# Layer 0 attention: a head's output projection in two stacked products instead of three, a DMA filling the upper half of the second operand

## What is computed

```python
kv_nope, kv_rope = (kv[..., :KV_LORA], kv[..., KV_LORA:])     # KV_LORA = 64
kvu = (kv_nope @ Wkv_up.T + bkv_up).reshape(b, s, NH, QK_NOPE + V_HEAD)...
scores = jnp.einsum('bhqd,bhkd->bhqk', q, k) / np.sqrt(Q_HEAD)
attn = jax.nn.softmax(scores, axis=-1)
o = jnp.einsum('bhqk,bhkv->bhqv', attn, v)
out = jnp.einsum('bhsv,Hv->bsH', o, Wo) + bo
```

## Time and profile before

| | |
|---|---|
| device time, median of 3 runs | 1565.31 us (1564.77 to 1566.88) |
| span of the profiled execution | 1564.7 us |
| time beside the span | no time of its own is listed for the profiled execution; its span lies 0.1 us under the fastest run |
| TensorE busy | 1503.2 us, 96% of the span |
| VectorE, ScalarE, GpSimd busy | 70%, 49%, 30% |
| attention heads of layer 0 | first scores at 39 us, last projection at 403 us |

### The profile page before, as it was taken

The page is one execution under the profiler, slowest core; times in us unless marked ns, Lnnn a source line. Parts: engine busy times, 40 slices in busy tenths (PEclk is TensorE's granted clock), DMA queues, the critical chain, the costliest instruction groups (busy, mean ns, idle before and its releaser), DMA issues. The chain is left out here.

```text
span 1564.7 us, 29168 instructions
## 1 busy us (share of the span) xinstructions
PE 1503.2 (96%) x9057; PEld 1320.1 (84%) x9057; DVE 1098.6 (70%) x2790; ACT 771.0 (49%) x2153; POOL 475.6 (30%) x505
## 2 busy tenths in 40 slices
PE   6999999999689989999999999999999999999898
PEld 5899999998367777888889888888888888988776
DVE  3788888888486756666676666666666667666765
ACT  3777878787345534434444444344443444444521
POOL 3445454545231013113213213312311321321321
PEclk9999999999799999999999999999999999999999
DMA  4111111111144440111011011011011101100001
GB/s 162 37 57 46 55 48 53 52 49 46 55 140 145 133 148 8 48 54 39 15 54 54 0 54 54 0 54 54 12 41 54 44 9 54 54 0 13 1 14 41
DMA packets 42833, 80.20 MB, mean 51 GB/s; under 512 B 5040, under 2 KB 13744, under 8 KB 42800
## 3 DMA queue, kind: packets, MB, share of 16 engines
q1 hardware_dynamic: 42800, 79.77, 16.8%
HBM read 77.66 MB, written 2.10 MB: 51 GB/s over the span
## 5 line engine op out<-in xcount | busy, mean ns | idle before, releaser
L98 PE MATMUL c_bj<-g_xT_hi,b_w 128*128 128x512 f32 x512 | 214.6, 419 | 2.8 <-PEq L901 2.8
L99 PE MATMUL c_bj<-g_xT_lo,b_w 128*128 128x512 f32 x512 | 203.3, 397 | 0.0
L100 PE MATMUL c_bj<-g_xT_hi,b_w 128*128 128x512 f32 x512 | 203.0, 397 | 0.0
L438 POOL TENSOR_TENSOR h_pr<-h_pr,h_rinv 128x512 f32<-128x512 f32 x128 | 133.2, 1041 | 159.9 <-DVE h_rinv L529 157.5
L1119 POOL CAST b_w<-b_raw_q 128x512 fp32r<-128x512 f32 x32 | 20.5, 640 | 435.8 <-PE c_bj L100 435.8
L98 PE MATMUL c_bj<-b_w,g_xT_hi 128*128 128x256 f32 x512 | 143.2, 280 | 0.0
L99 PE MATMUL c_bj<-b_w,g_xT_hi 128*128 128x256 f32 x512 | 143.2, 280 | 0.0
L100 PE MATMUL c_bj<-b_w,g_xT_lo 128*128 128x256 f32 x512 | 142.7, 279 | 0.0
L468 ACT ACTIVATE h_pr<-h_bs,h_nmax 128x256 f32<-128x256 f32 x256 | 118.8, 474 | 3.0 <-DVE h_nmax L524 2.1
L1351 DVE TENSOR_TENSOR c_v_lo<-c_bj,c_v_hi 128x256 fp32r<-128x256 f32 x128 | 54.3, 424 | 93.9 <-ACT c_v_hi L1263 93.9
L1247 ACT ACTIVATE c_o<-c_bo 128x128 f32<-128x128 f32 x128 | 35.5, 277 | 171.2 <-PE c_bo L1465 171.2
(11 more groups left out here) (266 smaller groups left out, 4663.8 us busy)
## 6 DMA issues: line engine op xcount, KB each, us to landing
f_wi<-in_w_ffn SPq DMA_DIRECT2D x66, 256.0 KB, 2.6
h_part<-in_w_ffn SPq DMA_DIRECT2D x32, 264.0 KB, 2.8
b_raw_q<-in_w_attn SPq DMA_DIRECT2D x32, 256.0 KB, 6.8
b_raw_k<-in_w_attn SPq DMA_DIRECT2D x32, 256.0 KB, 7.3
b_raw_v<-in_w_attn SPq DMA_DIRECT2D x16, 512.0 KB, 7.6
b_raw_o<-in_w_attn SPq DMA_DIRECT2D x16, 512.0 KB, 3.9
a_w<-in_w_head SPq DMA_DIRECT2D x32, 225.0 KB, 2.8
e_wraw<-in_w_ffn SPq DMA_DIRECT2D x1, 2304.0 KB, 8.4
```

The lines of the kernel that those rows point to most:

```text
L98: pe.matmul(out, w[0], x[0], start=start, stop=False, skip_group_check=True)
L99: pe.matmul(out, w[0], x[1], start=False, stop=False, skip_group_check=True)
L100: return pe.matmul(out, w[1], x[0], start=False, stop=stop, skip_group_check=True)
L438: pool.tensor_tensor(pr[b][:, :, :], pr[b][:, :, :], rinv[b][:, :][:, :, None].to_broadcast([P, 2, S]), ALU.mult)\
```

## The change

Each projection becomes two products. The first is hi times hi over all 128 rows, as before. The second uses two stacked operands: `wv_mix` has the rounded weights in rows 0 to 63 and their remainder in rows 64 to 127, and `o{i}_mix` has the remainder of the output's rows 0 to 63 in its lower half and a copy of the rounded rows 0 to 63 in its upper half. So hi times lo and lo times hi are added in one product. The cross terms of rows 64 to 127 (which are themselves a lo part) are left out. The copy across partitions is a DMA from `o_hi` to `o_mix`, issued by SyncE. Projections move from rounds b0 and b2 to b1 and b3, and `split_wv` from b1 to b2.

```diff
-        wvs = (t.sb("wv_hi", [P, VH], F32R), t.sb("wv_lo", [P, VH], F32R))
+        wvs = (t.sb("wv_hi", [P, VH], F32R), t.sb("wv_mix", [P, VH], F32R))
...
-        o = [(t.sb(f"o{i}_hi", [P, HALF], F32R), t.sb(f"o{i}_lo", [P, HALF], F32R)) for i in range(2)]
+        o = [(t.sb(f"o{i}_hi", [P, HALF], F32R), t.sb(f"o{i}_mix", [P, HALF], F32R)) for i in range(2)]
...
             round_(NH + 1, 0)
+            round_(NH + 1, 1)
...
                 def fetch_wv(h):
-                    need(sp, s_wvl, h)
+                    need(sp, s_wvl, 2 * h)
...
-                def both(h):
-                    fetch(h + 1)
-                    fetch_wv(h)
-                    fetch_part(h)
-
-                loop(sp, NH - 1, both)
-                fetch_wv(NH - 1)
-                fetch_part(NH - 1)
+                def duplicate(p, par):
+                    sp.wait_ge(s_ohi, p + 1)
+                    sp.dma_start(f32(o[par][1][KVL:P, :]), f32(o[par][0][0:KVL, :])).then_inc(s_odup[par], 16)
+
+                def ahead(h):
+                    if has(h - 3, NH):
+                        duplicate(2 * h - 6, 0)
+                    if has(h, NH):
+                        fetch(h)
+                    if has(h - 2, NH):
+                        fetch_wv(h - 2)
+                    if has(h - 3, NH):
+                        duplicate(2 * h - 5, 1)
+                    if has(h - 1, NH):
+                        fetch_part(h - 1)
+
+                fetch(1)
+                fetch_part(0)
+                ahead(2)
+                with sp.Fori(3, NH) as h:
+                    ahead(h)
+                for h in range(NH, NH + 3):
+                    ahead(h)
...
-                    pool.tensor_tensor(wvs[1][:, :], wv[:, :], f32(wvs[0][:, :]), ALU.subtract).then_inc(s_wvl, 1)
+                    plain(pool, s_tick)
+                    pool.tensor_copy(wvs[1][0:KVL, :], wv[0:KVL, :]).then_inc(s_wvl, 1)
+                    pool.wait_ge(s_wvl, 2 * h + 1)
+                    pool.tensor_tensor(wvs[1][KVL:P, :], wv[KVL:P, :], f32(wvs[0][KVL:P, :]), ALU.subtract)\
+                        .then_inc(s_wvl, 1)
+                    pool.wait_ge(s_wvl, 2 * h + 2)
...
-                    if b == 1 and has(h - 1, NH):
+                    if b == 2 and has(h - 1, NH):
                         split_wv(h - 1)
...
-                    dve.tensor_tensor(o[par][1][:, :], bo[:, :], f32(o[par][0][:, :]), ALU.subtract)\
+                    dve.tensor_tensor(o[par][1][0:KVL, :], bo[0:KVL, :], f32(o[par][0][0:KVL, :]), ALU.subtract)\
                        .then_inc(s_olo, 1)
...
-                    pe.wait_ge(s_wvl, h + 1)
-                    matmul3(pe, acc[c][:, :], (wvs[0][:, :], wvs[1][:, :]), (o[c][0][:, :], o[c][1][:, :]), False,
-                            False).then_inc(s_om, 1)
+                    pe.wait_ge(s_odup[c], 16 * (h + 1))
+                    pe.wait_ge(s_wvl, 2 * h + 2)
+                    pe.matmul(acc[c][:, :], wvs[0][:, :], o[c][0][:, :], start=False, stop=False,
+                              skip_group_check=True)
+                    pe.matmul(acc[c][:, :], wvs[1][:, :], o[c][1][:, :], start=False, stop=False,
+                              skip_group_check=True).then_inc(s_om, 1)
...
-                    if b == 0 and has(h - 2, NH):
+                    if b == 1 and has(h - 2, NH):
                         project(h - 2, 2 * h - 3, 1)
-                    if b == 2 and has(h - 1, NH):
+                    if b == 3 and has(h - 1, NH):
                         project(h - 1, 2 * h - 2, 0)
```

More of the change, by code:

```diff
@@ L372, in attention0_heads @@
         s_pv, s_ohi, s_olo = k.sem("pv"), k.sem("o_hi"), k.sem("o_lo")
-        s_wvh, s_wvl, s_om = k.sem("wv_hi"), k.sem("wv_lo"), k.sem("om")
+        s_wvh, s_wvl, s_om = k.sem("wv_hi"), k.sem("wv_mix"), k.sem("om")
+        s_odup = [k.sem(f"o_dup{i}") for i in range(2)]
         def run(eng, round_):
```

## The result

The changed kernel takes 1575.89 us (median of 4 runs), against 1565.8 us for the kernel before in the same comparison: 1.0057 times, 95% interval 1.0042 to 1.0072, or about +9 us. The change makes the kernel slower; the forecast was +6.4 us, to 1571.7 us. Both medians, 1575.9 us and 1574.4 us in the second comparison, lie inside the range of 1567.5 to 1576.5 us, the first near its upper end.

The account below looks back on a forecast made before the run. ScalarE's exponentials were taken to hold round b2 at 2.34 us, TensorE's work the other rounds. Loop +6.8, head 1 +0.5 and tail -0.9 gave +6.4 us, 1571.7 us; range 1567.5 to 1576.5 us, about 0.8.

Parts of the forecast that it names:

- The limit of round b2: Round b2: b3's scores wait for ScalarE's exponentials, so it stays 2.34 us and removing its 0.70 us projection wins nothing.
- the chain: ScalarE in b2: query rounding, probability rounding, then exponentials, 2.09 us from 0.20 us after the round's start; unmoved by the change.
- The faster rival: Round b2: exponentials don't hold b3, so the hole closes; 1554.7 us, or 1550 to 1552 with no limit; chance 0.10.
- Rounds b1 and b3 pay in full: Each gains two products, 0.47 us, with nothing else bounding its length: b1 3.36 us, b3 3.35 us.
- Round b0 wins its 0.70 us: Round b0 loses its projection and falls from 3.00 to 2.30 us, the normalization being ready just in time.
- The second rival: Round b0's transposes wait for GpSimd's normalization, the margin being 0.02 us: 0.1 us a pass, +2.9 us, 1574.6 us; chance 0.10.
- The pass: One loop pass of four rounds: 11.35 us against 11.11; over 29 passes +6.8 us.
- The copies and the split: Copies inside SBUF land after 2.1 us, the longer weight split takes at most 1.3 us; neither is waited for in the loop.
- The clock: Idle times in each pass lower TensorE's granted clock to 0.98 in the loop: up to 6.6 us, 1578 us; chance 0.03.
- The tail: Behind the loop: -0.6 earlier transposes, -1.28 last values, +1.4 copy wait, -0.43 product saved; together -0.9 us.
- The sum: Whole kernel: 6.8 + 0.5 - 0.9 = +6.4 us on a 1564.7 us span, plus 0.6 for the median: 1571.7 us.
- the likeliest case: Whole kernel: one added product a pass, end of the head stage as forecast; 1569 to 1574.5 us; chance 0.68.

Follow-up runs that it names:

- second comparison: The changed kernel, nothing edited, timed once more against the kernel before: 1.0045 (1.0032 to 1.0058); the kernel before against itself gave 1.0002.
- the repeat: The kernel before, nothing edited, run and profiled once more against itself: 1.0002 (0.9992 to 1.0011).
- second pair: Profiles of the kernel before and the changed kernel, both run again with nothing edited: 1.0002 and 1.0045 of the kernel before.

## Why the prediction was right

**The limit of round b2.** Right, and the step on which all hangs. I had read 2.34 us from rows 4 and 5; it is 2.34 in the changed kernel, with three products moved, and with the projection left out, and falls by 0.49 us when the chain becomes 0.49 us shorter. It is shown from both sides. The faster rival, that TensorE alone sets the pace, is out: 96 products could be taken away without effect.

**Rounds b1 and b3 pay in full.** Right: 3.35 us were measured for each, for the 3.36 and 3.35 predicted.

**Round b0 wins its 0.70 us.** Right: 2.32 or 2.30 us for 2.30. No wait on the normalization is listed there, so the margin of 0.02 us held; with so thin a margin that is in part luck. The second rival didn't come, though the run without b0's projection shows the wait where I had placed it.

**The pass.** 11.36 for 11.35 us. Up to the start of head 31 TensorE is 7.6 us behind the kernel before (391.37 against 383.74), where my sum had 7.3.

**The copies and the split.** Right. 2.2 us to landing where I took 2.1, between the rows of the loads; the estimate from the Trainium skill ("DMA: Bandwidth & Descriptors", anatomy of one DMA), 2.3 us, lies as far from it on the other side, though the section states its fit for DMAs that GpSimd issues and SyncE issues this one. Neither the copies nor the split is waited for in the loop. The third GpSimd instruction takes 0.29 us on 64 rows, my upper bound.

**The clock.** The rival didn't come: with 0.6 to 0.8 us idle in each pass the granted clock was 1.00 from 200 to 300 us.

**The tail.** The mis-sized term. I said -0.9 us. In the first pair of profiles it is -2.1 us: 7.6 us behind at head 31, and 5.6 us (409.31 against 403.74) at the first read of the sums. In the second pair it is -0.3 us: 7.5 us behind at head 31 (391.59 against 384.07), and 7.3 us (409.54 against 402.28) at the end. What parts the two pairs is TensorE's clock in the kernel before. The first read of the sums and the last 7.7 us of the head stage, in its first profile:

```profile
403.74 1.26 ACT L701 ACTIVATE o_os<-a_acc,g_bvs 128x512 f32<-128x512 f32 x2 [2.73 <-PEq L389]
...
396.00:403.70 7.70, 4.64 (x14) 3.26 (x14) 1.98 (x3) 1.60 (x3) 0.00 (x0) 0.62 0.00 0
```

and in the repeat, with the first product of the last projection, which had 0.79 us in the earlier trace rows:

```profile
401.01 0.50 PE L98 MATMUL a_acc<-h_o_hi,h_wv_hi 128*128 128x512 f32 x1 [1.41 <-DVE h_o_lo L538]
...
402.28 1.27 ACT L701 ACTIVATE o_os<-a_acc,g_bvs 128x512 f32<-128x512 f32 x2 [2.04 <-PEq L389]
...
394.60:402.30 7.70, 3.96 (x22) 2.98 (x22) 1.98 (x3) 1.70 (x4) 1.13 (x3) 1.00 0.00 0
```

The same code had a granted clock of 0.62 once and of 1.00 once. From the start of head 31 to the first read of the sums it takes 20.00 us in the first profile and 18.21 in the repeat; in the changed kernel it takes 17.94 and 17.95. The step that I had wrong is that I took the low clock of one profile for a property of the place, and priced there the projection that delayed the last values (1.28 us) and the product saved (0.43 us). Where both kernels ran at the full clock, in the second pair, the parts are these: -1.5 us up to the end of the last rounding for my -1.9, +1.5 us for the copy (2.30 us from the rounding to the projection, against 0.77) for my +1.4, and -0.3 us for the last products (1.01 us to the read of the sums, against 1.27) for my -0.4. Whether the change itself makes a low clock in the tail less likely stays open.

**The sum.** The device time of each run of the changed kernel is 1.75 to 1.85 us above its span, so the span of 1564.7 us that I started from most likely belongs to a run of about 1566.5 us, above the median and not below it; the sum was made on differences and isn't touched. +6.4 us were predicted, +7 to +9 measured, with intervals from 5 to 11. The head stage gives 5.6 us and, in the second pair, 7.3. In the first pair of profiles the later stages add 4.7 us that come and go with their clock. That the first median, 1575.9 us, is still inside the range is in part luck: it lies above the 1574.5 us up to which I had put the likeliest case, though that case's mechanism is what happened. Whether a part of the time in the later stages belongs to the shift in time stays open. In the eleven profiles, whose kernels share that code, it lies between 1161.0 and 1166.0 us and doesn't follow the time at which the stages start: 1166.0 at 398.5 us, 1161.0 at 403.2 and at 409.5, 1165.7 at 409.3.

## What to carry to other kernels

An engine that is shown busy all the time isn't for that the one that sets the pace of every part of a loop. Go round by round and ask what releases its first instruction; where work just fills a wait, taking it out brings nothing, and putting it elsewhere costs its whole length. The place to look is a stretch of the same loop that lacks the cover: here the unrolled head 0, whose round b2 (2.43 us) was as long without the work as that of the loop (2.34 us) with it.

When a saving is lost in such a wait, look at the order on the engine that releases it before cutting more work. Here two instructions changed places on ScalarE, with VectorE's made to fit, and then the product taken out of b2 counted.

A price read where the clock isn't full should be read from a second profile of the same kernel as well: here the last head took 20.0 us in one and 18.2 in the other.

## What was not expected of the hardware

- SyncE's queue shows 0.47 us for the issue of a copy from SBUF to SBUF of 64 rows of 2 KB, where the loads from HBM have medians of 0.33 to 0.39 us in the same profile.
- GpSimd's cast to F32R takes 287 ns on 64 x 128 and 289 ns on 128 x 128; the number of partitions doesn't show in it.
- The same code, in later stages of the same kernel, took 1161.0 or 1164.8 us, the longer time where the stretches in which TensorE waits a lot had the lower granted clock (0.72 and 0.89, against 0.81 and 1.00); its last head took 20.0 or 18.2 us at 0.62 or 1.00. So two profiles of one kernel differ by some 4 us in its later stages, more than half of what was to be measured here.
